# Attention and mixture of experts on one core: the products with V of a tile in one run of the tensor engine, behind the first scores of the next step

## Time and profile before

| what | before |
|---|---|
| median of 3 runs | 789.8 us (787.73 to 799.6) |
| the profiled execution | 793.8 us, span 792.0 us |
| tensor engine busy | 697.4 us, 88% of the span |
| VectorE, ScalarE, GpSimd busy | 428.2, 299.1, 111.1 us |
| chain that ended last | tensor engine 73% |
| mean granted clock of the tensor engine | 0.918 of full speed |
| line 550, products with V | 736 matmuls, mean 674 ns, merged 105.2 us |

### The profile page before, as it was taken

One profiled execution on the slowest core, in us unless ns is written; L12 is line 12 of the kernel. 1 busy time (PEld: TensorE's weight loads), 2 busy tenths in 40 slices (PEclk: granted clock), 3 DMA queues, 4 the chain that ended last, 5 costly groups with the idle time before them and its releaser, 6 DMA issues.

```text
span 792.0 us, 12810 instructions
## 1 busy us (share of the span) xinstructions
PE 697.4 (88%) x4836; PEld 464.1 (59%) x4836; DVE 428.2 (54%) x1026; ACT 299.1 (38%) x456; POOL 111.1 (14%) x198
## 2 busy tenths in 40 slices
PE   3065887999999999999899997999999999999995
PEld 2033444445444454454354445788888888888884
DVE  0051464644663756556646753376565665665666
ACT  3002354554554535544435673252222222222221
POOL 3010003431503012113102021100000000000000
PEclk9999998897997868987779998999999999999998
DMA  3919209029044070160260000000000000000000
GB/s 80 97 32 202 34 9 115 37 64 94 2 63 44 10 89 9 38 41 2 47 32 2 2 3 0 1 1 1 14 1 14 14 1 14 1 14 1 14 1 27
DMA packets 73740, 25.19 MB, mean 32 GB/s; under 512 B 64208, under 2 KB 68816, under 8 KB 73552
## 3 DMA queue, kind: packets, MB, share of 16 engines
q1 hardware_dynamic: 73680, 24.37, 22.5%
HBM read 16.24 MB, written 6.29 MB: 28 GB/s over the span
## 4 chain that ended last, share of the span: by engine, by line
PE 73%; DVE 8%; issue 6%; SPq 5%; DMA 4%; ACT 2%; POOL 1%; DVEq 0%; ACTq 0%; POOLq 0%
PE pX L674 14%; PE pV L550 12%; PE pX L658 8%; PE pX L660 7%; PE pX L659 7%; PE pX L514 5%; PE pX L475 4%; DVE rden L916 4%; SPq L316 3%; PE pM L596 3%; PE pX L505 2%; DMA q<-stage 2%; PE pV L572 2%; PE pX L526 2%; PE pM L558 2%
## 5 line engine op out<-in xcount | busy, mean ns | idle before, releaser
L874 DVE TENSOR_REDUCE mp<-pX 128x4 f32<-128x1024 f32 (+4 forms) x128 | 151.6, 1188 | 200.0 <-PE pX L479 154.7
L730 ACT ACTIVATE probs<-pX 128x1024 f32<-128x1024 f32 x152 | 154.8, 1019 | 158.5 <-PE pX L505 111.2
L777 ACT ACTIVATE probs<-pX 128x512 f32<-128x512 f32 x128 | 76.6, 599 | 195.4 <-PE pX L660 195.3
L951 DVE TENSOR_TENSOR probs<-probs,pX 128x512 f32<-128x512 f32 x128 | 87.5, 684 | 114.4 <-PE pX L660 110.9
L674 PEld LDWEIGHTS pX<-wd_sb,probs 128*128 128x128 f32 x1024 | 124.1, 192 | 5.3
L674 PE MATMUL pX<-wd_sb,probs 128*128 128x128 f32 x1024 | 124.4, 275 | 0.0
L550 PE MATMUL pV<-probs,vx 128*32 128x512 f32 (+1 forms) x736 | 105.2, 674 | 1.5 <-DVE z L928 1.5
L514 PE MATMUL pX<-q,kx 50*128 50x512 f32 x248 | 67.4, 540 | 21.6 <-DMA q<-stage 21.5
L475 PE MATMUL pX<-kx,q 48*128 48x512 f32 (+4 forms) x256 | 67.6, 530 | 20.4 <-DMA q<-q_scr 20.2
L475 PEld LDWEIGHTS pX<-kx,q 48*128 48x128 f32 x256 | 27.5, 213 | 83.8 <-issue 65.5
L960 DVE SCALAR_TENSOR_TENSOR z<-pX,wt,z 128x128 f32<-128x128 f32 x256 | 71.7, 343 | 1.4 <-PE pX L674 1.4
(11 more groups left out here) (106 smaller groups left out, 804.8 us busy)
## 6 DMA issues: line engine op xcount, KB each, us to landing
q<-q_scr SPq DMA_DIRECT2D x48, 128.0 KB, 6.9
xt<-xT SPq DMA_DIRECT2D x8, 512.0 KB, 4.8
q_scr<-qh SPq DMA_DIRECT2D x8, 256.0 KB, 2.0
q_scr<-ql SPq DMA_DIRECT2D x8, 256.0 KB, 2.1
out<-z SPq DMA_DIRECT2D x8, 256.0 KB, 2.3
kx<-kh SPq DMA_DIRECT2D x64, 16.0 KB
wd_sb<-wd SPq DMA_DIRECT2D x1, 1024.0 KB, 11.7
q<-stage SPq DMA_DIRECT2D x64, 4.0 KB
```

What stands on the lines that cost most here:

```text
L730: act.activation(dst, src[:], ACT.Exp).then_inc(exp_done, 1)
L777: act.activation(sg[:, n % 2, :], pX[0][:, n % 2, :], ACT.Silu).then_inc(sg_done, 1)
L874: dve.tensor_reduce(mp[:, t % 2, 0, :, i, :], src[:, :, 0:2 * n].rearrange("p r (c v k) -> p r v c k", v=NV, k=32), AX.XY, ALU.max).then_i ...
L951: dve.tensor_tensor(hid[:, n % 4, :], sg[:, n % 2, :], pX[1][:, n % 2, :], ALU.mult).then_inc(h_done, 1)
```

## The change

Round 0 of a tile's products with V no longer stands at the end of the tile's own step. All rounds of the tile stand together in the next step, behind A0 and B0, where rounds 1 and 2 already stood. The products, their number, their order among themselves and all waits inside `values` stay as they are. The step order becomes A0, B0, rounds 0, 1 and 2 of the tile before, A1, and so on to B4. The last tile's round 0 moves from the end of step 31 to step 32.

```
@@ def step(s) of the tensor engine
                 a_item(s + 2, 0)
                 b_item(s, 0)
                 if has(s - 1):
-                    for n in range(1, len(rounds(s - 1))):
+                    for n in range(len(rounds(s - 1))):
                         values(s - 1, n)
                 a_item(s + 2, 1)
...
                 for n, what in projected(s):
                     project(n, what)
                 b_item(s, 4)
-                if has(s):
-                    values(s, 0)
```

## The result

The changed kernel takes 812.66 us (median of 4, 808.65 to 817.26), the kernel before 794.7 us (median of 4, 787.73 to 804.84). The ratio is 1.0305, with a 95% interval of 1.0209 to 1.0401: slower by 3%, outside the forecast range of 780 to 806. The profiled execution took 812.61 us, its span 810.8 against 792.0 before, 18.8 us more.

A forecast was written before the change was run, and what follows sets the result against it. The prediction took the attention stage as bound by the tensor engine's order of work, its clock and its few waits. Saving -4.3, waits +6.0 and clock +1.5 gave +3.2 on 789.8: 793.0 us, range 780 to 806.

The forecast's parts named there:

- The clock term: Attention steps: round 0 comes later behind each step's thin end; one more 3.4 us half-clock stretch, +1.5 us (-6 to +9).
- The second rival: From a step's `sums` to round 0: longer thin part adds a slow stretch every second step, 22 us, 814 us; chance 0.12.
- the sentence that A0 and B0 fill the place as well as round 0: Slow stretch at 201.60 us: it ended with round 0, A0, B0 inside; the same instructions reordered would fill it as well.
- The sign of being wrong that was set: Mean clock from 78 to 478 us moving over 0.04, called a dozen stretches, or B0 waiting in every step.
- The first rival: Products with V in one run keep the clock up: a third of slow stretches gone, -18 us, 773.5 us; chance 0.06.
- The saving: Products with V: one run takes 2.29 us in place of 2.43, 0.14 us less in 31 steps, -4.3 us.
- the cover that was costed at nothing: B0 behind A0: VectorE's maximum of A4 frees its bank just in time; 0 us, or 3 us if not.
- the bound: Most the joined run could save: 0.25 us a step, -7.8 us, with A0 directly behind B4's mask.
- The waits: B0 waiting for the DMA from `stage`, no longer covered by round 0: +6.0 us (3.7 to 7.5).
- the third wait: B0's DMA wait of 0.93 us before 138.66 us: round 0 at half clock, 1.86 us, added in full.
- The forecast of no change: Whole kernel: 793.0 us, +3.2 us, no change that can be told; chance 0.60.

## Why the prediction was wrong

**The clock term was mis-sized; this is the failure.** The prediction took one slow stretch more, +1.5 us, within -6 and +9. The traces show some 14 more, about 21 us at that price, and with the waits taken out of both orders 18 to 20 us of the 24 are still there. The second rival had both the mechanism and the time: 814 us, measured 812.66. That the time fits to 1 us is in part luck: it took 22 us of clock, -4.3 and +6.0, and of the last two only the kind is borne out, not the size. The step that failed is the sentence that A0 and B0 fill the place as well as round 0, and the choice of +1.5 us "by the direction of the argument". The rows to do better were there: a late step at 1.00 and a like one at 0.86 say that these steps stand at the edge, and a change that acts on all 31 steps at an edge is not worth one stretch. The three late steps went from 1.00 to 0.77. (The sign of being wrong that was set, a clock moved by more than 0.04, came: 0.85 to 0.80. But 0.04 over 400 us are nine stretches, not a dozen.) Shown is that work in the thin part or right behind it brings the clock back and the same work in the dense part doesn't; what it is in the thin part that makes the clock fall, its length or its kind of work, was not taken apart.

**The first rival fell.** The run of 24 records did not keep the clock up, which is 0.80 for 0.85; in the late step shown it is lost before the run starts. The rule of the Trainium skill cited there ("TensorE: Matmul & The Clock Gate", section Loop structure matters more than you think), to keep matmuls dense and free of long gaps, bears on the thin part here rather than on the dense run: 0.75 us of idle matmuls there gained 36 us. The gaps that they filled were of some 0.4 us, no long ones, and the thin part was busy 2.98 of 3.40 us when the clock fell.

**The saving was right as a size and came in some steps only.** 2.28 us for the run, forecast 2.29. In plain steps B0 waits 0.3 us for VectorE's maximum of A4, and the step stays at 10.15 us: there the term is 0, and the cover that was costed at nothing gave way. In steps with a K projection the saving is 0.31 to 0.33 us, more than the 0.25 of the bound, as A0 also starts sooner behind the mask. Such steps could be compared at full clock in few places, so the sum over all steps isn't measured; it isn't 0, and -4.3 may be near.

**The waits grew by more than forecast, and what they cost stays open.** +2.0 and +2.1 us at 83 and 123 us came, the third wait vanished, none came at 175, and three came later that weren't placed; in all B0 waited 10.4 us longer, where +6.0 stood. The error was to take the length of a wait as its cost in time. By 145 us only 0.4 us were lost, where 3.7 stood, and the 4.23 us before 306.82 cost nothing, since the tensor engine had come there sooner: such a wait ends with the DMA, not with the engine. Between the orders without these waits the distance is 4 to 6 us smaller than with them, no more than the runs can tell.

**The forecast of no change** was thus wrong by the clock in the main. The waits and the saving together came to little, as it said (with idle work the two orders are equal), but by two terms that cancel and that these runs can't size one by one.

## What to carry to other kernels

In this kernel, with the tensor engine's granted clock between its two levels over the stage, the order of its work moved the clock, and this was a first-order term. Where a profile looks like that, ask of every move which part of the step gets thinner and how near it is to losing the clock, and price a repeated edge by all steps, not by one. Test it with a dry copy of the moved work at its old place: if added work costs nearly nothing, look how much of it fell into waits, and what is left speaks for the clock. Split a difference of two traces into busy time and the rest before pricing it; a longer wait need not be a loss. And work that is useless but lies where the engine waits anyway can pay for itself: six small matmuls a step, with a DMA issue moved off a crowded queue, gave 4% here (four gave nearly as much), while the queue move alone gave nothing.

## What the runs showed of the hardware that was not expected

Added matmuls can make a program faster: 776.73 us with four more a step against 812.66 without. The same four at a dense place made it slower, 830.6 us. The place of the dense work counts more than its amount: with the same matmuls in three orders the compared time was 788.6 (round 0 at the step's end), 812.7 (all together) and 842.3 us (in three places), at mean clocks of 0.85, 0.80 and 0.75. And removing the waits for one DMA (41.2 us of them in one kernel, 14.9 before the first scores of the transposed kind) gained 15 and 19 us with the clock up, and nothing with the clock in between, where other waits and a lower clock took their place.
